# Adjacency blocks of 64 destinations with both relations in one PSUM bank, and degrees summed from the finished matrix

## What is computed

```
for r in range(NUM_RELATIONS):
    gate = jax.nn.sigmoid(x_j @ gate_w[r, :, 0])
    msgs.append(gate[:, None] * x_j @ w[r])
msg = jnp.where((edge_type == 0)[:, None], msgs[0], msgs[1])
agg = jax.ops.segment_sum(msg, row, num_segments=x.shape[0])
...
deg = jax.ops.segment_sum(jnp.ones((E,), x.dtype), edge_index[1], num_segments=N)
agg = agg / jnp.maximum(deg, 1.0)[:, None]
```

## Time and profile before

| | us |
|---|---|
| median of 3 runs | 808.13 |
| the runs | 807.37 to 809.75 |
| the profiled execution | 807.63 |
| its span in the profile | 805.9 |
| TensorE busy | 783.2 (97%) |
| VectorE busy | 632.0 (78%) |
| ScalarE busy | 293.2 (36%) |
| GpSimd busy | 67.3 (8%) |

### The profile page before, as it was taken

One profiled execution on the slowest core, in us unless ns is written; L12 is line 12 of the kernel. 1 busy time (PEld: TensorE's weight loads), 2 busy tenths in 40 slices (PEclk: granted clock), 3 DMA queues, 4 the chain that ended last, 5 costly groups with the idle time before them and its releaser, 6 DMA issues.

```text
span 805.9 us, 10950 instructions
## 1 busy us (share of the span) xinstructions
PE 783.2 (97%) x3899; PEld 623.4 (77%) x3899; DVE 632.0 (78%) x918; ACT 293.2 (36%) x545; POOL 67.3 (8%) x74
## 2 busy tenths in 40 slices
PE   5999999999999999999999999999999999999997
PEld 4998757867477777477776878897898888888886
DVE  6867999999999999994968454338778865886863
ACT  4453214235411013124142633123445544545541
POOL 3100010220200000000401260030000000000000
PEclk9999999998999999999999999999799999999999
DMA  7600779796898786622041130008133231133101
GB/s 252 239 1 34 228 235 333 247 280 211 249 293 290 245 274 239 229 85 105 0 167 37 70 105 1 1 2 209 53 117 100 71 105 53 53 105 106 53 1 64
DMA packets 68268, 111.67 MB, mean 139 GB/s; under 512 B 4305, under 2 KB 21582, under 8 KB 68220
## 3 DMA queue, kind: packets, MB, share of 16 engines
q1 hardware_dynamic: 62426, 100.51, 37.5%
q0 software_dynamic: 2880, 5.12, 3.7%
q10 hardware_dynamic: 2914, 5.41, 1.8%
HBM read 107.18 MB, written 1.28 MB: 135 GB/s over the span
## 4 chain that ended last, share of the span: by engine, by line
PE 90%; DVE 6%; issue 2%; ACT 1%; DVEq 1%; DMA 0%; SPq 0%; ACTq 0%
PE bank L1643 54%; PE bank L2110 11%; PE bank L1712 6%; PE bank L1862 4%; PE bank L1881 3%; PE bank L1874 2%; PE bank L1855 2%; PE bank L1969 2%; PE bank L1650 2%; PE bank L1761 1%; PE bank L2044 0%; DVE ew_lo L1514 0%; DVE slot L1589 0%; DVE tmp L1099 0%; PE bank L1847 0%
## 5 line engine op out<-in xcount | busy, mean ns | idle before, releaser
L1186 DVE SCALAR_TENSOR_TENSOR weights<-weights,att 128x2048 f32<-128x2048 f32 x116 | 263.4, 2343 | 0.7
L1643 PE MATMUL bank<-half,ew_hi 128*128 128x314 f32 (+1 forms) x456 | 102.8, 314 | 3.3 <-DVE slot L1580 2.0
L1643 PE MATMUL bank<-AT,slot 125*128 125x312 f32 (+1 forms) x400 | 105.8, 426 | 0.0
L1643 PEld LDWEIGHTS bank<-AT,slot 125*128 125x128 f32 x400 | 75.6, 189 | 30.4 <-issue 1.3
L1643 PE MATMUL bank<-weights,slot 128*125 128x512 f32 (+5 forms) x306 | 84.8, 438 | 2.3 <-ACT slot L914 1.6
L1643 PEld LDWEIGHTS bank<-half,ew_hi 128*128 128x128 f32 x456 | 78.5, 193 | 8.1 <-DVE slot L1580 2.8
L1643 PEld LDWEIGHTS bank<-weights,slot 128*125 128x125 f32 (+2 forms) x306 | 50.5, 198 | 30.5 <-issue 26.7
L1643 PE MATMUL bank<-half,ew_lo 128*128 128x314 f32 (+1 forms) x228 | 70.8, 311 | 0.0
L1643 PE MATMUL bank<-slot,weights 128*128 128x313 f32 (+2 forms) x304 | 68.2, 384 | 0.7 <-ACT slot L834 0.7
L676 ACT ACTIVATE slot<-bank 125x512 f32<-125x512 f32 (+7 forms) x62 | 31.2, 538 | 97.6 <-PE bank L1643 87.2
L1643 PEld LDWEIGHTS bank<-slot,weights 128*128 128x128 f32 x304 | 50.9, 193 | 16.8 <-issue 1.3
(11 more groups left out here) (340 smaller groups left out, 1222.7 us busy)
## 6 DMA issues: line engine op xcount, KB each, us to landing
weights<-in_L_gnn_basis SPq DMA_DIRECT2D x60, 1024.0 KB, 5.4
weights<-in_L_ffn_W SPq DMA_DIRECT2D x31, 512.0 KB, 4.4
weights<-in_L_ffn_W SPq DMA_DIRECT2D x16, 256.0 KB, 5.3
weights<-in_L_mix_kqv_w SPq DMA_DIRECT2D x1, 3072.0 KB, 10.3
weights<-in_w_qkvT SPq DMA_DIRECT2D x3, 1024.0 KB, 6.5
slot<-slot POOLq DMA_DIRECT2D x10, 250.0 KB, 7.9
weights<-in_L_mix_mlp_w ACTq DMA_DIRECT2D x2, 1024.0 KB, 17.8
weights<-in_L_gnn_root ACTq DMA_DIRECT2D x2, 1024.0 KB, 10.2
```

What stands on the lines that cost most here:

```text
L1186: ins = dve.scalar_tensor_tensor(wrel[layer][r], wmat(at), att[:, layer, r, b:b + 1], wrel[layer][r], ALU.mult, ALU.add)
L1643: ins = pe.matmul(out, a, b, start=i == 0, stop=i == len(pairs) - 1)
```

## The change

The matrix is made in ten blocks, two to each tile of 125 destinations: 64 and 61 destinations (`BLOCKS`, `BH`). Both relations of a block stand in one bank, relation 0 in partitions 0 to 63 and relation 1 in 64 to 127, so a block has two banks (one for each half of the sources), and a column of edges two matmuls with one weight of 128 columns. `oh_dst` is 128 wide. Instead of a key per block there is an iota per block (`iota_dst`, ten of them, made by GpSimd) with the block's start folded in. `EU`, the number of columns in a group and of slots in a ring, goes from 4 to 2. The range computation handles ten blocks and 40 groups, in two `rng` banks. Semaphores `oh_used` and `oh_ready` are shared by blocks b and b + 5, so from block 5 on both engines load a third register (a second on TensorE), the number of groups that block b - 5 had. ScalarE copies four pieces for each block (64 or 61 partitions by 312 or 313) without sums; the degrees are one reduction over the summed matrix.

```
-EU = 4
+EU = 2
...
+BLOCKS, BH = 2 * TT, 64
+A_BLOCK = [("A0", 0), ("A0", 2), ("A0", 4), ("A0", 6), ("A2", 0), ("A2", 2), ("A3", 0), ("A3", 2), ("A", 0), ("A", 2)]
...
-        oh_dst = [[ring[:, 876 * u + 626:876 * u + 876] for u in range(EU)] for ring in (oh, oh2)]
+        oh_dst = [[ring[:, 876 * u + 626:876 * u + 754] for u in range(EU)] for ring in (oh, oh2)]
...
-            pool.iota(iota_dst, pattern=[[1024, 2], [1, P]], base=0, channel_multiplier=0,
-                      allow_small_or_imprecise_dtypes=True).then_inc(S("consts"), 1)
+            for b in range(BLOCKS):
+                ins = pool.iota(iota_dst[:, b, :], pattern=[[1024, 2], [1, BH]], base=P * (b // 2) + BH * (b % 2), channel_multiplier=0,
+                                allow_small_or_imprecise_dtypes=True)
+            ins.then_inc(S("consts"), 1)
...
-                for q in range(4):
-                    r, (a, w) = q // 2, HALF[q % 2]
-                    copy_out(stage, n + q, AT[:, r, j, a:a + w], B(stage, n + q)[0:P, 0:w], accum_out=deg_part[:, j, q:q + 1])
+                for hf, (a, w) in enumerate(HALF):
+                    act.wait_ge(S("psum_full"), filled(stage, n + hf + 1))
+                    for r in range(2):
+                        ins = act.activation(AT[at:at + rows, r, j, a:a + w], B(stage, n + hf)[BH * r:BH * r + rows, 0:w], ACT.Copy)
+                    ins.then_inc(S("act_read"), 1)
...
-            for j in range(TT):
-                ins = dve.tensor_scalar(keyf[:, j, :], relf, -float(P * j), None, ALU.add)
-            link(ins)
...
-            for j in range(TT):
-                groups = dve.value_load(rng_i[0:1, j:j + 1], min_val=1, max_val=EG)
-                q0 = dve.value_load(rng_i[0:1, 5 + j:6 + j], min_val=0, max_val=EG - 1)
-                if j > 1:
-                    dve.wait_ge(S("psum_full"), filled(A_BLOCK[j - 2][0], A_BLOCK[j - 2][1] + 4))
+            for b in range(BLOCKS):
+                groups = dve.value_load(rng_i[0:1, b:b + 1], min_val=1, max_val=EG)
+                q0 = dve.value_load(rng_i[0:1, BLOCKS + b:BLOCKS + b + 1], min_val=0, max_val=EG - 1)
+
+                past = dve.value_load(rng_i[0:1, b - TT:b - TT + 1], min_val=1, max_val=EG) if b >= TT else 0
+                if b > 1:
+                    dve.wait_ge(S("psum_full"), filled(A_BLOCK[b - 2][0], A_BLOCK[b - 2][1] + 2))
                 with dve.Fori(0, groups) as i:
                     for u in range(EU):
-                        dve.wait_ge(S(f"oh_used{j}"), EU * i + u + 1)
...
+                        dve.wait_ge(S(f"oh_used{b % TT}"), EU * (past + i) + (u + 1 + (EU if b >= TT else 0)))
+                        dve.tensor_scalar(oh_src[b % 2][u], iota_src, small[0:P, bass.ds(EU * q0 + EU * i + u, 1)], None, ALU.is_equal)
+                        dve.tensor_scalar(oh_dst[b % 2][u], iota_dst[:, b, :], small[0:P, bass.ds(EU * q0 + EU * i + (560 + u), 1)], None,
+                                          ALU.is_equal).then_inc(S(f"oh_ready{b % TT}"), 1)
...
-            link(dve.tensor_reduce(deg, deg_part[:, :, :], AX.X, ALU.add))
+            link(dve.tensor_reduce(deg, AT[:, 0, :, :], AX.X, ALU.add))
...
-                        for bkq, r, (a, w) in parts:
-                            ins = pe.matmul(bkq[0:P, 0:w], oh_dst[j % 2][u][:, P * r:P * r + P], oh_src[j % 2][u][:, a:a + w],
-                                            start=False, stop=False)
-                        ins.then_inc(S(f"oh_used{j}"), 1)
+                        for bkq, a, w in parts:
+                            ins = pe.matmul(bkq[:, 0:w], oh_dst[b % 2][u], oh_src[b % 2][u][:, a:a + w], start=False, stop=False)
+                        ins.then_inc(S(f"oh_used{b % TT}"), 1)
```

More of the change, by code:

```diff
@@ L1715, in _ @@
[L1715 to L1717 removed]
+                        pe.wait_ge(S(f"oh_ready{b % TT}"), EU * (past + i) + (u + 1))
+                        for bkq, a, w in parts:
+                            ins = pe.matmul(bkq[:, 0:w], oh_dst[b % 2][u], oh_src[b % 2][u][:, a:a + w], start=False, stop=False)
+                        ins.then_inc(S(f"oh_used{b % TT}"), 1)
@@ L1718, in _ @@
+                for bkq, a, w in parts:
+                    pe.matmul(bkq[:, 0:1], zero[:, 0:128], zero[:, 0:1], start=False, stop=True).then_inc(S("psum_full"), 1)
+                if b == 3:
                     pe.wait_ge(S("consts"), 1)
```

109 lines of the change are left out of this document (54 added, 55 removed).

## The result

The changed kernel takes 839.43 us (median of 4 runs, 838.18 to 840.67) against 807.83 us of the kernel before (807.37 to 809.75) on the same chip: a ratio of 1.039, 95% interval 1.037 to 1.040, or 31.6 us more. The forecast was 829.3, the range 817 to 846. The sign, the ring and the loads came out as predicted. The forecast's own case did not: what happened is rival 1, the low clock, at the place between 829 and 843 that the prediction left for it. The time lies in the range because the range was drawn to take in that rival.

A forecast was written before the change was run, and what follows sets the result against it. The prediction took TensorE, busy 783.2 of 805.9 us, to bound the kernel. To the profiled 807.63 us it added 21.4 for the later end of the adjacency stage and 0.3 for the degrees: 829.3, range 817 to 846.

The forecast's parts named there:

- The sign: Whole kernel: the change makes it slower, chance 0.92, against faster 0.05 and same 0.03.
- the ring: One-hot stage: with two slots VectorE waits for a slot's release, 1.31 us in 39 groups, 51.1 us.
- the loads: Block starts: register loads are paid in the open, 2.35 us for blocks 1 to 4, 3.1 for 5 to 9.
- The forecast's own case: Adjacency stage: slot waits and block starts bind, low clock in only three rounds; 829.3 us, chance 0.57.
- rival 1: Adjacency stage: TensorE's clock falls to 1.2 GHz for most of it, rounds of 1.53 us; 843 us, chance 0.26.
- the one of 2.35: Block starts 1 to 4: 2.35 us each from last source to first of the next block, 9.4 us in all.

The follow-up runs named there:

- e10_warm_const: The changed kernel with 28 zero-weight matmuls ahead of the first pair and constants in place of the register loads; 810.88 us.
- e3_warm: The changed kernel with 28 zero-weight matmuls of 312 columns run once, ahead of the first pair; 836.93 us.
- e6_before_ring2: The kernel before with a ring of two slots instead of four, its five blocks and four matmuls a pair kept; 825.74 us.

## What to carry to other kernels

Size a ring by the time in which one slot comes round (fill, wait for the consumer, use, release), not by the rates of the two engines: here a round of 1.27 us over a pace of 0.46 asks for three slots by this sum (three were not run, four were enough), and halving both the consumer's work and the slots turned a hidden release into 39 waits. Whoever makes more and shorter loops pays the loop's entry each time, register loads first, and should price it from rows: here the traced start of 1.93 us was the right price and the one of 2.35, which I took, too dear. And where TensorE is made the engine that waits, ask at which clock it will wait: an engine that reached the high clock while it was the bottleneck may not get there any more, and then its remaining matmuls start at half the rate; look at the distance of matmul starts, not at the clock column.

## What the runs showed of the hardware that I had not expected

- The same bursts can hold a high clock and don't raise a low one: 0.55 us of matmuls in every 1.20 to 1.27 us held 2.4 GHz for a whole stage at the shorter round (e10_warm_const) and for block 0 at the longer (e3_warm), while 1.05 us of matmuls in every 1.54 us left it at 1.2 GHz for 50 us (the changed kernel). It rose after stretches without gaps: 28 matmuls ahead of block 0, 16 transposes, or 3.95 us of 4 busy. What lowers it is shown only in part: the falls mostly came at or behind long block starts, one came after two rounds of 1.27 us, ahead of a start.
- The granted clock reads 1.00 up to the first change recorded. The changed kernel has 12 records in 4 us at a granted 1.00 (20 to 24 us) and 12 at a granted 0.50 (72 to 76 us).
- Two register loads cost 1.3 us between the sources at a block's start and a third 0.62, one behind another. An address that is a sum with a loaded register adds about 0.08 us to a round in which the engine waits (1.27 against 1.20 at the high clock, 1.54 against 1.45 at the low one), as it is made after the release.
- From the start of TensorE's last matmul on a slot to VectorE's next instruction it is 0.53 us at the high clock, the same for two (e3_warm, 20.13 to 20.66) and for four matmuls a pair (e6_before_ring2, 34.14 to 34.67), and 0.70 at the low one (the changed kernel, 19.86 to 20.56); these two rings of two slots paid it in every round.
- VectorE's reduction over 125x3125 took 3.41 us beside GpSimd's work, as long as the addition of that size ahead of it, while the 5-element step behind it took 3.02 us and ended with GpSimd's instruction.
